# The attention product of a two-layer graph kernel as a split product of three passes

## What is computed

```
# layer 0                                       # layer 1
q, k = split(x @ Wqk);  v = x @ Wv              query, key, value = x @ W.T + b   (three of them)
agg = adj @ (k * mask)                          weight = adj * exp(query @ key.T)
w = (q . agg) / 16, per node                    weight = weight / sum(weight, axis=2)
L = softmax(w over the nodes) * v               L = weight @ value
x = layernorm(x + L)                            x = layernorm(x + L)
```

## Time and profile before

| | us |
|---|---|
| median of 3 runs (lowest, highest) | 326.86 (326.02, 327.0) |
| the profiled execution, its own time | 324.46 |
| the profiled execution, its span | 322.6 |

### The profile page before, as it was taken

How to read it: one execution, slowest core, us unless ns; L and a number is a source line. 1 busy time by engine, 2 the same in 40 slices (tenths; PEclk the granted TensorE clock), 3 DMA queues, 4 the chain that set the end, 5 groups by cost and what they waited for, 6 DMA issues and landing times. The chain is left out here.

```text
span 322.6 us, 6510 instructions
## 1 busy us (share of the span) xinstructions
PE 304.7 (94%) x1894; PEld 271.0 (84%) x1894; DVE 220.6 (68%) x688; ACT 200.8 (62%) x455; POOL 142.0 (44%) x177
## 2 busy tenths in 40 slices
PE   7878999999999999999999999999999999999770
PEld 6557889999898889999988899998988899999660
DVE  1346877777777777777778777777777777767652
ACT  2435557766666667666666677666666676666562
POOL 1354444455553444455543344555543344553312
PEclk9999999999999999999999999999999999999996
DMA  7811221233433322234333222233333222210002
GB/s 246 291 56 44 82 83 50 81 102 114 117 114 114 99 76 84 82 113 114 114 114 114 82 81 86 93 114 114 114 114 103 80 79 83 78 51 35 33 35 98
DMA packets 19021, 31.26 MB, mean 97 GB/s; under 512 B 2112, under 2 KB 6336, under 8 KB 19008
## 3 DMA queue, kind: packets, MB, share of 16 engines
q1 hardware_dynamic: 19008, 31.11, 31.1%
HBM read 22.71 MB, written 8.39 MB: 96 GB/s over the span
## 5 line engine op out<-in xcount | busy, mean ns | idle before, releaser
L244 POOL TENSOR_TENSOR rstd<-var_eps,minus_half 128x4 f32<-128x4 f32 x35 | 35.7, 1019 | 159.7 <-ACT x L301 86.2
L301 ACT ACTIVATE x<-x_sum,shift,rstd 128x256 f32<-128x256 f32 x64 | 35.0, 595 | 48.6 <-POOL shift L247 48.6
L504 PE MATMUL ps<-w_hi,xt_hi 128*128 128x512 f32 x128 | 61.6, 481 | 0.1
L506 PE MATMUL ps<-w_hi,xt_lo 128*128 128x512 f32 x128 | 50.5, 395 | 0.0
L505 PE MATMUL ps<-w_lo,xt_hi 128*128 128x512 f32 x128 | 50.2, 393 | 0.0
L252 POOL TENSOR_TENSOR xt_lo<-xt_raw,xt_hi 128x512 fp32r<-128x512 f32 x31 | 40.2, 1296 | 7.3 <-ACT xt_hi L295 7.3
L268 POOL TENSOR_TENSOR x1b<-x,bv_all 128x512 f32<-128x512 f32 x32 | 41.3, 1289 | 2.4 <-ACT x L301 2.4
L378 DVE CUSTOM_DVE_ANT_0 agg<-ps,agg,adjt 128x256 f32<-128x256 f32 x64 | 31.0, 484 | 12.9 <-issue 8.0
L504 PE MATMUL ps<-wv_hi,x1t_hi 128*128 128x258 f32 x128 | 38.8, 303 | 0.0
L351 ACT ACTIVATE z<-ps,z_bias 128x256 f32<-128x256 f32 x64 | 26.8, 470 | 16.4 <-PE ps L506 16.4
L301 ACT ACTIVATE x<-x,shift,rstd 128x256 f32<-128x256 f32 x64 | 34.9, 595 | 3.2 <-POOL shift L247 3.2
(11 more groups left out here) (77 smaller groups left out, 644.7 us busy)
## 6 DMA issues: line engine op xcount, KB each, us to landing
xt_raw<-xt_pairs SPq DMA_DIRECT2D x32, 256.0 KB, 2.7
x_raw<-x_pairs SPq DMA_DIRECT2D x32, 256.0 KB, 2.7
out_pairs<-x SPq DMA_DIRECT2D x32, 256.0 KB, 2.0
adjt<-adjt_pairs SPq DMA_DIRECT2D x32, 129.0 KB, 2.1
p<-params SPq DMA_DIRECT2D x1, 770.0 KB, 6.9
p<-params SPq DMA_DIRECT2D x1, 512.0 KB, 3.7
p<-params SPq DMA_DIRECT2D x1, 256.0 KB, 5.5
bv_all<-value_bias SPq DMA_DIRECT2D x1, 128.0 KB, 7.5
```

Of the source, the lines that this page charges most:

```text
L244: nc.gpsimd.tensor_tensor(rstd[r % 2][:, :, :], var_eps[:, :, :], minus_half[:, :, :], ALU.pow)\
L301: last = nc.scalar.activation(out[:, graph(g)], in_[:, graph(g)], ACT.Identity, bias=shift[r % 2][:, layer, g:g + 1], scale=rstd[r % 2][:, ...
L504: nc.tensor.matmul(out, s_hi, m_hi, start=(n == 0), stop=False)
L506: mm = nc.tensor.matmul(out, s_lo, m_hi, start=False, stop=(n == len(parts) - 1))
```

## The change

The attention product goes through `split_product` as well. For that both operands get a rounded part and a remainder:

- ScalarE's copy of the values out of PSUM writes `val_hi` (rounded) in place of `val`. It is the same instruction in the same place.
- VectorE forms `val_lo` = values in PSUM minus `val_hi`, straight behind `edge`.
- ScalarE forms `edge_hi`, the rounded `edge`, between its copies of `x1t` and of `agg`. It waits for `edge_done`.
- GpSimd forms `edge_lo` = `edge` minus `edge_hi` at the start of its slot, ahead of `rstd`. It waits for `edge_hi_done`.
- TensorE waits for `edge_lo` and `val_lo` in place of `edge` and `val`, and issues six float32r matmuls in place of two float32 products.
- VectorE's next `edge` also waits for `edge_lo` of the pair before.

```diff
@@ GpSimd's slot
             def slot(t, r):
+                if exists(t - 1):
+                    pool.wait_ge(edge_hi_done, t)
+                    nc.gpsimd.tensor_tensor(edge_lo[:, :], edge[:, :], edge_hi[:, :].bitcast(F32), ALU.subtract)\
+                        .then_inc(edge_lo_done, 1)
                 if exists(t + 1) or exists(t - 2):
@@ ScalarE's slot
                     nc.scalar.copy(x1t[:, :, :, :], x1t_ps).then_inc(x1t_copied, 1)
+                if exists(t - 1):
+                    act.wait_ge(edge_done, t)
+                    if exists(t - 2):
+                        act.wait_ge(sum_done, t - 1)
+                    nc.scalar.copy(edge_hi[:, :], edge[:, :]).then_inc(edge_hi_done, 1)
...
-                    nc.scalar.copy(val[:, :, 0:DIM], val_ps[:, :, 0:DIM]).then_inc(val_copied, 1)
+                    nc.scalar.copy(val_hi[:, :, 0:DIM], val_ps[:, :, 0:DIM]).then_inc(val_copied, 1)
@@ VectorE's slot
                     if exists(t - 2):
+                        dve.wait_ge(edge_lo_done, t - 1)
                         dve.wait_ge(sum_done, t - 1)
                     nc.vector.tensor_tensor(edge[:, :], exp_s[:, :], adjt[(r - 1) % 4][:, 0:PAIR_N], ALU.mult)\
                         .then_inc(edge_done, 1)
+                    nc.vector.tensor_tensor(val_lo[:, :, 0:DIM], val_ps[:, :, 0:DIM], val_hi[:, :, 0:DIM].bitcast(F32),
+                                            ALU.subtract).then_inc(val_lo_done, 1)
@@ TensorE's slot
-                    pe.wait_ge(edge_done, t)
-                    pe.wait_ge(val_copied, t)
-                    for g in range(2):
-                        mm = nc.tensor.matmul(sum_ps[:, g, 0:VAL_COLS], edge[:, graph(g, NODES)], val[:, g, :],
-                                              start=True, stop=True)
+                    pe.wait_ge(edge_lo_done, t)
+                    pe.wait_ge(val_lo_done, t)
+                    for g in range(2):
+                        mm = split_product(sum_ps[:, g, 0:VAL_COLS], [(
+                            edge_hi[:, graph(g, NODES)], edge_lo[:, graph(g, NODES)], val_hi[:, g, :], val_lo[:, g, :])])
```

More of the change, by code:

```diff
@@ L88, in build @@
         z = sb("z", [128, HALVES, PAIR_N])
-        val = sb("val", [128, 2, VAL_COLS])
+        val_hi = sb("val_hi", [128, 2, VAL_COLS], F32R)
+        val_lo = sb("val_lo", [128, 2, VAL_COLS], F32R)
         score_bias = sb("score_bias", [128, 2])
@@ L92, in build @@
         edge = sb("edge", [128, PAIR_N])
+        edge_hi = sb("edge_hi", [128, PAIR_N], F32R)
+        edge_lo = sb("edge_lo", [128, PAIR_N], F32R)
         den_inv = sb("den_inv", [128, 2])
@@ L143, in build @@
         first_xt_lo_done = sem("first_xt_lo_done")
+        edge_hi_done, edge_lo_done, val_lo_done = sem("edge_hi_done"), sem("edge_lo_done"), sem("val_lo_done")
         xt_lo_done, adjm_done, x1b_done = sem("xt_lo_done"), sem("adjm_done"), sem("x1b_done")
@@ L278, in _ @@
             nc.gpsimd.memset(wv1_lo[:, :, DIM:VAL_COLS].bitcast(F32), 0.0)
-            nc.gpsimd.memset(val[:, :, DIM:DIM + 1], 1.0)
-            nc.gpsimd.memset(val[:, :, DIM + 1:VAL_COLS], 0.0).then_inc(consts_ready, 1)
+            nc.gpsimd.memset(val_hi[:, :, DIM:DIM + 1].bitcast(F32), 1.0)
+            nc.gpsimd.memset(val_hi[:, :, DIM + 1:VAL_COLS].bitcast(F32), 0.0)
+            nc.gpsimd.memset(val_lo[:, :, DIM:VAL_COLS].bitcast(F32), 0.0).then_inc(consts_ready, 1)
             pool.wait_ge(ident_zeroed, 1)
```

## The result

| | before | after |
|---|---|---|
| median of the runs compared (lowest, highest), us | 326.93 (326.02, 329.05) | 340.61 (339.12, 342.29) |
| the profiled execution: its own time, its span, us | 324.46, 322.6 | 342.29, 340.5 |

The changed kernel takes 1.041 of the time before (95% interval 1.034 to 1.048).

A forecast was written before the change was run, and what follows sets the result against it. TensorE's own work was taken to bound the kernel at 9.13 us a slot. VectorE's loop, grown to 9.53, adds 28 x 0.40 = 11.2, the last slots 3.0: 338.7 on the profiled execution, stated as 340.5, range 328 to 350.

The forecast's parts named there:

- the one over `x1t_hi` and L600: VectorE's loop with TensorE: 8.47 us plus 0.59 for `val_lo` plus 0.47 of hold, 9.53 a slot against 9.13.
- the rival's: VectorE's `x1t_hi` goes first, `edge_lo` waits; the product's loop takes 9.62 us, up to 9.8; 347 us; chance 0.20.
- the terms on TensorE: Six float32r matmuls take 0.72 us against 0.89, saving 0.17 a slot; TensorE's own work comes to 8.96.
- the added steps: ScalarE's `edge_hi` 0.41 us, GpSimd's `edge_lo` 0.65 (0.55 to 0.75), VectorE's `val_lo` 0.67.
- the two would meet: VectorE's `x1t_hi` (154.61) and GpSimd's `edge_lo` (154.63) come at the same moment in every slot, and one stands still.
- If it is held until GpSimd lets go: VectorE's `x1t_hi` stands still until 0.20 us before `edge_lo` ends, losing 0.47 us a slot (bounds nothing to 0.75).
- just about hidden: GpSimd's later `x1b` and `adjm` lie over VectorE's `p_row`, at a cost of 0 to 0.2 us.
- the sum: 28 slots at 0.40, 11.2 us, plus 3.0 in the last three slots: 324.46 + 14.2 = 338.7, stated as 340.5.
- Neutral: `x1t_hi` and `edge_lo` miss each other or the cast isn't held; the pace stays; 329 us (326 to 332); chance 0.15.
- the loop through the product: `edge`, `edge_hi`, `edge_lo`, product: the start 0.1 to 0.2 us late eats the 0.17 saved; closes at about 9.13.
- The faster case: No meeting, `edge_lo` ready by about 155.2, L600 catching up 0.1; TensorE's 8.96 sets the pace; 324 us; chance 0.06.

The follow-up runs named there:

- e8: Changed kernel, VectorE reordered: `edge` between the two `x1_sum`, `stats` ahead of `x1t_hi`, second `weight` ahead of `den_inv` and `x2`, `neg_max` earlier; 325.8 us.
- e7: Changed kernel with its steps and waits, but the product as two plain float32 matmuls, the remainders unused; 347.3 us.
- e1: Changed kernel with VectorE's `stats` of `x1_sum` moved between `val_lo` and `x1t_hi`, all work kept; 334.1 us.
- e9: e8 with the old float32 product in the last three slots, without `edge_hi`, `edge_lo` and `val_lo` there; 322.3 us.
- e6: Kernel before the change, with VectorE reordered: `edge` between the two `x1_sum`, `stats` ahead of `x1t_hi`; 326.1 us.
- e10: e9 with the old float32 product in the first three slots with a product too; 321.9 us.
- e3: Changed kernel without VectorE's `val_lo`; the second pass uses the rounded values again; 345.3 us.
- e4: Changed kernel with GpSimd's `edge_lo` replaced by a subtract of 128x4 and a memset of an unused tile; third pass uses rounded edges; 338.4 us.

## Why the prediction was right or wrong, point by point

**The number** was 0.1 us off the median and the range held. That was luck. The forecast named the wrong loop: the one over `x1t_hi` and L600, at 9.53 us a slot. The loop that does bind is the rival's, through the product, and I had put that at 9.62. It came out at 9.51, next to the forecast. The sizes helped as well: the 27 slots cost 10.0 in place of 11.2, and both ends together more than the 3.0 that I had for them.

**Right: the terms on TensorE.** A slot without waits is 8.96 us (e8), as worked out; e7 gives 0.16 for the product.

**Right: the added steps but one.** `edge_hi` 0.41 (forecast 0.41), `val_lo` 0.68 (0.67). `edge_lo` is 0.75 where nothing holds it, the far end of its bounds; I had taken 0.65, from half of `xt_lo` and from `adjm`. That costs 0.10 a slot, and e1 shows it bare.

**Right: that the two would meet, and with what sort of price.** The rows on `p_row` and `adjm` did foretell that a VectorE instruction on SBUF and a GpSimd one exclude each other, and that GpSimd lets go before its record ends: beside `edge_lo`, `x1t_lo` stood until 153.98 - 0.69 = 153.29, 0.14 ahead of `edge_lo`'s end (forecast 0.20). That `edge_lo` and `x1t_hi` would come within some hundredths of a microsecond of each other was right too.

**Wrong: who wins.** The step that failed is "If it is held until GpSimd lets go": I gave the tie to GpSimd, because the only rows I had show VectorE as the one that stands still. In those rows GpSimd was already at work (`x1b` until 32.71, `p_row` from 32.61). After the change the records of both begin within 0.01 us of each other, in the 31 slots in which both stand, and VectorE runs through in all of them (mean 416 ns) while `edge_lo` is held (1.01 us in place of 0.75). With that, the chain that binds is the rival's: the product waits, not L618.

**Wrong: the rival's price.** I had put it at 9.62 a slot and up to 9.8, and 347 us. The loop measured 3.05 + 6.21 + 0.25 = 9.51, against 3.08 + 6.29 + 0.25 = 9.62, so the price was 0.11 too high even at its lower end. `edge_lo` ends 0.60 behind `x1t_hi` and not 0.70, and TensorE's part is 6.21 and not 6.29. The upper end assumed that `x1t_lo`, held as well, would add to the slot. It is held, by 0.42, more than I had allowed for, and adds nothing, because VectorE's loop has 9.51 - 9.38 = 0.13 to spare even so. Likewise `p_row`, which `adjm` now holds to 0.76: this was to be "just about hidden", and is: it ends at 159.50, while TensorE's scores (L632) run until 159.75.

**Near: the sum.** Forecast 28 slots at 0.40, 11.2, and 3.0 for the last slots, 14.2 in all. Measured in the profiled pair 27 slots at 0.37, 10.0; then 4.7 behind the last `p_row` and 3.2 ahead of the steady slots, for which I had no term at all. By the medians, 13.7 less 10.0 leaves 3.7 for both ends. With the order of e8 the new steps cost 3.5 us in the last slots, by e8 and e9, part of it perhaps by the clock: the 3.0 was a little low. The share of the first slots went mostly with the clock and not with the steps (e6, e10), and the trace of before, at full clock there, shows nothing of it.

**The other rivals.** Neutral (329) would have been right had the two missed each other and `edge_lo` taken 0.65; e1, without the meeting, is at 334, since 0.75 is too long for it. The 9.13 that the prediction gives for the loop through the product doesn't follow from its own terms: by the rival's way of adding they make 155.34 - 152.63 = 2.71, 6.29 and 0.25, 9.25. e1, with 0.75, has 9.24, so 9.14 with 0.65: the sum was wrong and the figure still near, mostly as TensorE's part is 6.20 and not 6.29. The faster case was put at 324 and called for `edge_lo` ready in time, no meeting, and no wait at L600. e9 gets there by another order: in its steady slots `edge_lo` and `x1t_lo` take 0.74 and 0.69, its matmuls never wait for `edge_lo`, and it takes 322.3.

## What to carry to other kernels

Before giving GpSimd a step, write down which VectorE instruction will run beside it: one with two SBUF inputs, or a cast from SBUF to SBUF, and a GpSimd instruction that reads exclude each other, and the one that comes second loses nearly all that the first has left. `stats` of one SBUF tile and a subtract of PSUM and one tile cost nothing beside it, so moving one of them in between (e1) takes the meeting away; less work on VectorE without looking at who stands beside whom can make things worse (e3). And a loop that saves 0.17 us a slot has some 4.5 us to give over the 27 slots of this kernel, of which the slots at the end, where nothing covers the new steps, took 3.5 back: use the old form there.

## What the runs showed of the hardware that I had not expected

- When the records of `x1t_hi` and `edge_lo` start together (within 0.01 us, 31 slots), VectorE runs through: `x1t_hi` keeps 416 ns while `edge_lo` takes 1002 on the mean (e7: 419 and 1003; e4: 416, and 469 for 4 columns). That a tie goes to VectorE as a rule is not shown. In each of these slots VectorE comes straight from another instruction and GpSimd from standing still (2.47 us in the slot shown).
- The start of a record doesn't say who is held. `p_row` starts at 158.74, 0.07 ahead of `adjm` (158.81), and is the one that stands still, until `adjm` is nearly done (0.76 in place of 0.27). There it is GpSimd that comes straight from another instruction, `x1b`, whose record ends at 158.86. The earlier trace rows have the same at 32.61. Which of two such instructions asks first, these records can't tell.
- A GpSimd subtract of only 128x4 was held some 0.26 us by a VectorE cast (0.48 against 0.22, e4).
- A held GpSimd `edge_lo` ends 0.59 to 0.60 us behind the VectorE record that held it, though it needs 0.75 alone: the hold ends some 0.15 ahead of what the records show, in this direction as in the other (0.14 for `x1t_lo`).
- `edge_lo` (128x256, two full inputs, rounded output) takes 0.75 us where `adjm` of the same size takes 0.62.
